# Batch 0's K and Q copied straight into their rows by halves of the heads, Q's chain first, the preparation of a batch one loop earlier

## What is computed

```python
Q = (layernorm(x) @ w_q.T)   # 16 heads of 8
K, V = ctx @ w_k.T, ctx @ w_v.T
scores = Q K^T / sqrt(8);  scores = where(mask, scores, -inf)
x = x + (softmax(scores) V) @ w_o.T
h = silu(xn @ w_gate.T) * (xn @ w_up.T)      # xn = layernorm(x)
x = x + h @ w_down.T                         # int weights / 127
```

## Time and profile before

| | us |
|---|---|
| runs | 180.27, 185.03, 186.02 (median 185.03) |
| profiled execution | 182.24 |
| its span | 180.4 |
| PE busy | 165.1 (91%) |
| DVE busy | 134.4 (74%) |
| ACT busy | 109.9 (61%) |
| POOL busy | 63.4 (35%) |

### The profile page before, as it was taken

One profiled execution on the slowest core, in us unless ns is written; L12 is line 12 of the kernel. 1 busy time (PEld: TensorE's weight loads), 2 busy tenths in 40 slices (PEclk: granted clock), 3 DMA queues, 4 the chain that ended last, 5 costly groups with the idle time before them and its releaser, 6 DMA issues.

```text
span 180.4 us, 4294 instructions
## 1 busy us (share of the span) xinstructions
PE 165.1 (91%) x1630; PEld 103.6 (57%) x1630; DVE 134.4 (74%) x315; ACT 109.9 (61%) x231; POOL 63.4 (35%) x108
## 2 busy tenths in 40 slices
PE   5877999998998799999999999999899999999693
PEld 5556655554554346557655765575465546656583
DVE  6844579789499779868986889789978982533763
ACT  4434421985596588847866786677677746866130
POOL 8421655531307741971396058100500050000100
PEclk9996999999999999999999999999999999999999
DMA  4729989188059007803950593069100000100011
GB/s 150 270 64 204 243 144 239 52 219 140 0 145 202 11 8 216 136 0 93 222 79 0 143 198 47 4 187 174 25 2 29 5 0 2 33 2 0 4 60 29
DMA packets 17525, 17.06 MB, mean 95 GB/s; under 512 B 1536, under 2 KB 16128, under 8 KB 16832
## 3 DMA queue, kind: packets, MB, share of 16 engines
q1 hardware_dynamic: 17040, 16.12, 39.0%
q10 hardware_dynamic: 464, 0.67, 1.4%
HBM read 9.24 MB, written 7.34 MB: 92 GB/s over the span
## 4 chain that ended last, share of the span: by engine, by line
PE 68%; DVE 22%; ACT 2%; DMA 2%; issue 2%; ACTq 1%; SPq 1%
PE pv_bank L340 14%; DVE neg_max L818 12%; PE score_bank L280 11%; PE max_bank L297 5%; PE pv_bank L428 5%; PE ffn_bank L405 4%; PE ffn_bank L393 4%; PE ffn_bank L396 3%; PE post_bank L381 2%; DMA ctx_all<-ctxT 2%; PE prep_bank L319 2%; PE post_bank L357 2%; DVE x L896 2%; DVE stats L902 2%; PE prep_bank L311 2%
## 5 line engine op out<-in xcount | busy, mean ns | idle before, releaser
L818 DVE TENSOR_REDUCE neg_max<-max_bank 128x2 f32<-128x512 f32 x128 | 82.0, 684 | 15.6 <-PE max_bank L297 15.2
L613 ACT ACTIVATE probs<-score_bank 128x512 f32<-128x512 f32 x128 | 70.3, 598 | 22.0 <-PE score_bank L280 21.8
L297 PE MATMUL max_bank<-k_ops,q_ops 49*128 49x256 bf16 x256 | 43.2, 273 | 4.0 <-DVE neg_max L818 3.9
L280 PE MATMUL score_bank<-q_ops,k_ops 51*128 51x256 bf16 x256 | 42.8, 273 | 0.6 <-ACT probs L613 0.4
L340 PE MATMUL pv_bank<-probs,v_ops 128*32 128x256 f32 x480 | 32.5, 385 | 0.0
L280 PEld LDWEIGHTS score_bank<-q_ops,k_ops 51*128 51x128 bf16 x256 | 19.3, 94 | 19.5 <-ACT probs L613 9.1
L297 PEld LDWEIGHTS max_bank<-k_ops,q_ops 49*128 49x128 bf16 x256 | 16.7, 94 | 10.9 <-DVE neg_max L818 7.5
L1101 POOL CAST max_parts<-neg_max 128x16 bf16<-128x16 f32 x14 | 2.8, 198 | 54.9 <-DVE neg_max L818 54.9
L340 PEld LDWEIGHTS pv_bank<-probs,v_ops 128*32 128x32 f32 x480 | 13.7, 109 | 9.5 <-issue 4.0
L1108 POOL TENSOR_TENSOR rstd<-var,minus_half 128x2 f32<-128x2 f32 x8 | 5.6, 702 | 32.5 <-DVE var L915 32.5
L428 PE MATMUL pv_bank<-ident_bf 128*128 128x128 bf16 x150 | 14.7, 252 | 1.9 <-POOL ident_bf L1131 1.9
(11 more groups left out here) (139 smaller groups left out, 232.3 us busy)
## 6 DMA issues: line engine op xcount, KB each, us to landing
k_ops<-k_rows SPq DMA_DIRECT2D x7, 384.0 KB, 4.7
q_ops<-q_rows SPq DMA_DIRECT2D x7, 384.0 KB, 6.2
k_rows<-kq_parts SPq DMA_DIRECT2D x8, 192.0 KB, 2.1
q_rows<-kq_parts SPq DMA_DIRECT2D x8, 192.0 KB, 2.2
k_rows<-kq_parts SPq DMA_DIRECT2D x8, 128.0 KB, 2.1
q_rows<-kq_parts SPq DMA_DIRECT2D x8, 128.0 KB, 2.1
out<-y SPq DMA_DIRECT2D x7, 128.0 KB, 2.3
x_all<-x SPq DMA_DIRECT2D x1, 768.0 KB, 6.2
```

Of the source, the lines that this page charges most:

```text
L280: mm = pe.matmul(score_bank[k % 2][:, t * S:(t + 1) * S], rows(k_ops, b, ROWS)[:, k, t * P:(t + 1) * P], rows(q_ops, b, ROWS)[:, k, :], st ...
L297: mm = pe.matmul(max_bank[k % 2][:, t * S:(t + 1) * S], rows(q_ops, b, MAX_ROWS)[:, k, t * P:(t + 1) * P], rows(k_ops, b, MAX_ROWS)[:, k, ...
L613: act.activation(probs[:, k % RING].rearrange("p t s -> p (t s)"), score_bank[k % 2][:, :], ACT.Exp, scale=SCALE).then_inc(probs_ready, 1)
L818: dve.tensor_reduce(neg_max[:, b % 2, :, k], max_bank[k % 2][:, :].rearrange("p (t s) -> p t s", t=TT), AX.X, ALU.max, negate=True).then_i ...
```

## The change

Batch 0's K and Q no longer go through DRAM. `spread_half` copies one product group of one half of the heads from `kq_parts` (64 partitions of 256 elements) to 8 partitions of 8 heads in `k_ops` or `q_ops`: 24 copies, of which SP issues 22 and ACT 2. For a half of the heads to lie in 64 neighbouring partitions, the weights of batch 0 are permuted on ACT into `wkq_halves`. x 0 is loaded ahead of context 0. In the start, Q's chain stands ahead of work for batch 1 on DVE and ACT; on PE `keep_warm(18)` becomes 30 and the later counts 8, 8, 6, 20 stand for 16, 6, 6, 40. `x_all` is loaded by 2 to 3 and 4 to 7; context 2 and 3 stand behind all copies of batch 0 and all writes of batch 1 on SP. The fills of `v_ops[2]`, `v_ops[3]` move from ACT to POOL, that of `q_ops[1]` from DVE to ACT. The projections of batches 2 and 3 move from heads 6 and 14 to 9 and 15 of batch 0, and five heads have no warming matmuls. The preparation of batch b+4 now stands in loop b for b from 0 to 3 (before: b+3 for b from 1 to 4).

The core of the diff:

```diff
+        def spread_half(eng, side, part, n, g):
+            ops, groups, landed = ((q_ops, Q_GROUPS, q_half), (k_ops, K_GROUPS, k_half))[side]
+            first, stride, _ = groups[part]
+            row = DK * (first + stride * n)
+            eng.dma_start(rows(ops, 0, SPREAD)[row:row + DK, HALF * g:HALF * (g + 1)],
+                          kq_parts[HALF_ROWS * g:HALF_ROWS * (g + 1), 0, part, S * (1 - side):S * (2 - side)])\
+                .then_inc(landed[g], 16)
...
-            sp.dma_start(x_all[:, 2:B], x[:, 2:B]).then_inc(x_in[2], 16)
+            sp.dma_start(x_all[:, 2:4], x[:, 2:4]).then_inc(x_in[2], 16)
+            sp.wait_ge(k_filled[0], 1)
             for part, done in enumerate((k_part1, k_part2, k0_part3)):
                 sp.wait_ge(done, 1)
-                to_dram(0, 1, part)
-            for part, done in enumerate((q_part1, q_part2, q0_part3)):
-                sp.wait_ge(done, 1)
-                to_dram(0, 0, part)
+                for n in range(K_GROUPS[part][2]):
+                    spread_half(sp, 1, part, n, 0)
             sp.wait_ge(q_filled[0], 1)
-            sp.wait_ge(q_bounced[0], 16 * PARTS)
-            for g in range(2):
-                half_from_dram(sp, 0, g)
-            sp.dma_start(ctx_all[:, 2:4], ctxT[:, 2:4]).then_inc(ctx_in[2], 16)
+            sp.wait_ge(q_part1, 1)
+            for n in range(3):
+                spread_half(sp, 0, 0, n, 0)
+            sp.wait_ge(q0_part3, 1)
+            spread_half(sp, 0, 2, 0, 0)
+            for part in range(PARTS):
+                for n in range(K_GROUPS[part][2]):
+                    spread_half(sp, 1, part, n, 1)
+            sp.wait_ge(q_part2, 1)
+            for part in range(PARTS):
+                for n in range(Q_GROUPS[part][2]):
+                    spread_half(sp, 0, part, n, 1)
...
-            sp.wait_ge(k_filled[0], 1)
+            sp.dma_start(ctx_all[:, 2:4], ctxT[:, 2:4]).then_inc(ctx_in[2], 16)
             from_dram(sp, 1, 1)
...
             for k in range(HEADS):
                 max_head(0, k)
-                keep_warm(4, pv_bank)
-                if k == 3:
+                if k not in (6, 9, 10, 12, 15):
+                    keep_warm(4, pv_bank)
+                if k == 6:
                     turn_xn1(2, prep_bank)
-                if k == 6:
+                if k == 9:
                     pe.wait_ge(xn1_t_ready, 3)
                     project_k(2, prep_bank[:, 0:S])
                     project_q(2, prep_bank[:, S:2 * S]).then_inc(kq_proj, 1)
...
-                prep = 1 <= b < B - 3
+                prep = b < B - 4
...
+                    keep_warm(4, post_bank)
+                    pe.wait_ge(v_ready, 3)
+                    turn_xn1(4, prep_bank)
...
-            part1(0, 1, k_rest, kq_rest[:, 0:S], 0, k_part2)
-            part1(1, 0, k_proj, max_bank[0][:, 0:S], 0, k_part1)
-            copy_xn1_t(0, score_bank[1])
-            part1(0, 0, q_proj, ffn_bank[:, 0:S], S, q_part1)
-            part1(1, 1, k_rest, kq_f[:, 0:S], 0, k_part2)
-            part1(0, 1, q_rest, kq_rest[:, S:2 * S], S, q_part2)
             act.wait_ge(mask_ready, 1)
...
+            copy_xn1_t(0, score_bank[1])
+            part1(0, 1, k_rest, kq_rest[:, 0:S], 0, k_part2)
+            part1(0, 0, q_proj, ffn_bank[:, 0:S], S, q_part1)
+            part1(1, 0, k_proj, max_bank[0][:, 0:S], 0, k_part1)
+            part1(0, 1, q_rest, kq_rest[:, S:2 * S], S, q_part2)
+            act.wait_ge(q_filled[0], 1)
+            act.wait_ge(q_part2, 1)
+            for n in range(2):
+                spread_half(act, 0, 1, n, 0)
```

More of the change, by code:

```diff
@@ L182, in from_dram @@
             eng.dma_start(rows(ops, b, SPREAD).rearrange("r h s -> r (h s)"), dram[b].ap()).then_inc(landed[b], 16)
-        def half_from_dram(eng, side, g):
-            dram, ops, landed = ((q_rows, q_ops, q_half), (k_rows, k_ops, k_half))[side]
-            eng.dma_start(rows(ops, 0, SPREAD)[:, HALF * g:HALF * (g + 1)].rearrange("r h s -> r (h s)"),
-                          dram[0].ap()[:, HALF * S * g:HALF * S * (g + 1)]).then_inc(landed[g], 16)
+        def spread_half(eng, side, part, n, g):
[5 more added lines that the diff above has]
+                .then_inc(landed[g], 16)
         def spread_mask(eng, b):
@@ L310, in project_k @@
                 ctx_wait(pe, b)
[L311 removed]
+                return pe.matmul(to, (wkq if b else wkq_halves)[:, 0], ctx_all[:, b], start=True, stop=True)
             def project_q(b, to):
                 pe.wait_ge(xn1_t_ready, b + 1)
[L315 removed]
+                return pe.matmul(to, (wkq if b else wkq_halves)[:, 1], xn1_t[:, :], start=True, stop=True)
             def project_v(b, to):
@@ L993, in _ @@
                     output(b - 3, ffn_bank)
+                else:
+                    stats_of_x(b + 5)
+                    moments_of_x(b + 5)
+                    eps_of_x(b + 5)
                 head_max(b + 1, 4)
@@ L1002, in _ @@
                     hide(b - 2, 0, ffn_bank)
-                if b < 2:
-                    for c in range(2 * b + 4, 2 * b + 6):
-                        stats_of_x(c)
-                        moments_of_x(c)
-                        eps_of_x(c)
                 head_max(b + 1, 8)
@@ L1083, in split_kq @@
                 pool.wait_ge(kq_copied, b - 1)
-                pool.wait_ge(k_bounced[b - 2], 16 * PARTS)
-                pool.wait_ge(q_bounced[b - 2], 16 * PARTS)
+                if b == 2:
+                    for g in range(2):
+                        pool.wait_ge(k_half[g], 16 * PRODUCTS)
+                        pool.wait_ge(q_half[g], 16 * PRODUCTS)
+                else:
+                    pool.wait_ge(k_bounced[b - 2], 16 * PARTS)
+                    pool.wait_ge(q_bounced[b - 2], 16 * PARTS)
                 pool.tensor_copy(kq_parts[:, b % 2, 0], kq_f[:, :]).then_inc(part1_done, 1)
```

170 lines of the change are left out of this document (79 added, 91 removed).

## The result

The changed kernel takes 191.33 us (median of four executions, 189.07 to 191.58), the kernel before 182.82 (four, 180.27 to 186.02). The ratio is 1.058, with a 95% interval of 1.044 to 1.071: slower. I had predicted 186.0 with a range from 181 to 190. The profiled execution took 189.07 us, its span is 187.3 and its mean granted clock 0.918, against 182.24, 180.4 and 0.991.

A forecast was written before the change was run, and what follows sets the result against it. It took the start's chain to the first head, a bounce through DRAM, as the room left, TensorE being busy afterwards. Plus 3.4, minus 0.5, minus 0.4 gave plus 2.5 us on the mean 183.4: 186.0, range 181.0 to 190.0.

The forecast's parts named there:

- the sum: Whole kernel: loop opening plus 3.4, loop 0 minus 0.5, batch 4's loop minus 0.4, together plus 2.5 us.
- The issue's price: Start, SP's direct copies: 0.63 us from one issue to the next, with bounds 0.36 and 0.79.
- The rival of cheap issues: Start, SP's copies: an issue costs 0.37 to 0.5 us, context arrives earlier, 181.5 at 0.37; chance 0.25.
- The wait of 4.6 us for the context: Start, `project_k(2)`: TensorE, ready at 23.8, waits 4.6 us for context 2 and 3, landing at 28.4.
- The landing: Start, load of context 2 and 3: behind batch 1's writes, ending at 23.9, it takes 4.5 us, to 28.4.
- The clock: Behind the context wait: TensorE slows to its low clock, costing 2.0 us over two projections and four heads.
- The first head: Start, batch 0: first head at 15.0, 4.6 us earlier than 19.62; wider ends 14.2 and 17.
- Head 8: Start, batch 0: heads 0 to 7 end at 20.4, second-half copies land at 22.5, so head 8 waits 2 us.
- The loops: Loops over the batches: minus 0.5 us in batch 0's and minus 0.4 in batch 4's.
- a sign of error: Loops over the batches: the prediction is wrong if they shrink by more than 1 us.
- the 0.4: Batch 4's loop: it loses its preparation, 16.68 instead of 17.08 us, minus 0.4.
- fewer warming matmuls: Batch 0's loop: 32 fewer at 0.07 us, minus 2.2, against added turn and projections; minus 0.5 net.

The follow-up runs named there:

- the one that opens at 35.5: Changed kernel with batch 0's K and Q through DRAM again, weights not permuted, context 2 and 3 issued behind Q's reads: 185.74 us, ratio 1.011.
- the last two versions with direct copies: Changed kernel, early context and x, more warming, six Q copies on ScalarE's queue: 181.98 us; then w_ff's load there too: 179.42 us, ratio 0.987.
- the one before them: Changed kernel with context 2 and 3 and x 4 to 7 issued early and warming matmuls in TensorE's idle times: ratio 1.012.
- the last version: Changed kernel, early context and x, more warming, six Q copies and w_ff's load on ScalarE's queue: 179.42 us, ratio 0.987.

## Why the prediction was wrong, step by step

Against the profiled execution the sum said a span of 182.9 (180.4 plus 2.5); it was 187.3, 4.4 more. What was forecast to decide, a context load late behind SyncE's issues with TensorE waiting for it, did decide. Two terms of the sum failed: the landing of that load (4.5 us, measured 6.8) and how long TensorE stays slow (2.0 us of slow steps; about 4 measured, the whole way to the loops).

| step | predicted | measured |
| --- | --- | --- |
| an issue, from one to the next | 0.63 | 0.65 |
| K's first half issued | 7.0 to 10.8 | 6.1 to 10.2 |
| first head | 15.0 | 16.14 |
| second halves issued to | 20.9 | 21.3 |
| context 2, 3 issued | 23.9 | 24.54 |
| its landing | 4.5 | 6.8 |
| `project_k(2)` | 28.4 | 31.36 |
| from there to the loops | 7.7 | 9.75 |
| loops open | 36.1 | 41.11 |
| loops to the span's end | 146.85 | 146.2 |

- **The issue's price** was right: chosen by the shape of the mask and shift rows, not by the DRAM writes. The rival of cheap issues falls, and the context's load was late by the place that the sum gave it.
- **The wait of 4.6 us for the context** was 4.82, but by two errors that cancel. The heads ahead of it ended 2.7 us later than I said (26.5 instead of 23.8) and the load landed 3.0 us later.
- **The landing** is the term "23.9 plus 4.5". I took it from the context's landings in the kernel before, where no reads of K and Q stood right behind the load that it answers to (SyncE's next rows there are K's writes). Behind its new place stand batch 1's two reads, and holding them back gave 3.8 us. This mis-sized term is 2.3 of the 4.4 us; the late issue adds 0.6. Each landing is that of one trace.
- **The clock.** "I expect the 4.6 us to do the same", 2.0 us of slow steps behind the wait, was the failed step. It is wrong in two ways. The clock had fallen by 12 us, ahead of the first head, behind TensorE's idle times there, and not in the wait. And the step gave it back after four heads; it stayed at 0.50 up to the loops, so the stretch took 9.75 us: 2.05 us more. The second is what cost: with early context the stretch takes 9.8 with no wait ahead of it, and with 40 warming matmuls, where the clock did fall in the wait, 9.76. That it is the clock and not added work shows in the run with six copies on ScalarE's queue: at 1.00, without its wait for the shift rows, the stretch takes 6.35 us, with three more groups of warming matmuls in it.
- **The first head** was late by 1.1 us, not by Q, but by TensorE itself: behind V's projection (which waited 0.75 us for ScalarE) came the 20 warming matmuls, 2.34 us. I had followed Q's data and SyncE's list, and not counted TensorE's own work up to there. It cost nothing here, since the heads ended 4.8 us before the context was in.
- **Head 8** didn't wait, as heads at 1.08 us reach it only at 24.85. Where the clock was high in the first eight heads, with all 22 copies on SyncE, the wait was 1.4 to 2.4 us, about the 2 predicted.
- **The loops** gave 1.55 us instead of 0.9, over the 1 us that I had named as a sign of error. Batch 4's gave 0.23 for the 0.4. The rest is in loop 0 and what leads to the first `turn_pv`: 34.0 us from the opening (41.11 to 75.11), 35.4 before. The text put this on fewer warming matmuls; their removal alone gained nothing in the kernel before. It is tempting to say that a loop that opens late finds the other engines' preparation done: the bounced runs with TensorE kept busy, which open at 31.4 and 31.2, have a longer stretch (36.6 and 35.8) than the one that opens at 35.5 (34.0). But the last two versions with direct copies open at 31.4 and 31.0 and take 35.2 and 34.4, and the one before them opens at 34.5 and takes 37.1. So the cause of the 1.55 stays open.

In sum: plus 0.6 for the issue, 2.3 for the landing, 2.05 for the clock, minus 0.65 for the loops, 4.3 of 4.4. The median lies another 2.3 above the profiled execution, the fastest of the four, and I had added 1.3 for that; this 1.0 and the 4.4 are the 5.3 between 186.0 and 191.33, but for rounding.

Not settled: why the clock differs from trace to trace behind the same first 16 us of TensorE's instructions. In 16 to 20 it is 0.50 in the changed kernel and in two of its variants (early context; x and w_ff later), 0.79 with the reads held back and 1.00 with the load ahead of the writes. Nor is it shown that the direct copies are what wins in the last version: the bounce was not run with w_ff's load moved.

## What to carry to other kernels

Many small copies on one queue are paid by whatever is issued behind them: count every issue (0.6 us here), write down when the last load of the list goes out, and give the loads that have no condition a place ahead of those that have. Take a landing from a row in which the same transfers stand behind the load, not from one in which others do. Don't count on the clock coming back after a few heads. Where a step shortens a stretch at the start of a kernel, read the granted clock there, and check by a run with one wait taken away which of several waits is next before counting the gain.
